# Two stages of a fused attention kernel put into one block, with the key blocks of the first stage in other tiles

## The reference, cut to what matters

```python
x = x + cross_attention(layernorm(x), ctx)       # 16 heads of 128, 4 key heads, RMS norm on queries and keys, softmax
x = x + mixture_of_experts_0(layernorm(x))
x = x + linear_attention(layernorm(x), ctx, mask)  # 16 heads of 16: features relu(f(q)), relu(f(k)) of 64
x = x + mixture_of_experts_1(layernorm(x))
```

## Time and profile before

| | |
|---|---|
| time, median of 3 runs | 1274.75 us (1274.42 to 1274.98) |
| the profiled execution | 1277.79 us |
| its span | 1276.0 us |
| TensorE busy | 1190.6 us, 93% |
| VectorE busy | 879.2 us, 69% |
| ScalarE busy | 738.2 us, 58% |
| GpSimd busy | 536.0 us, 42% |

### The profile page before, as it was taken

The page is one execution under the profiler, slowest core; times in us unless marked ns, Lnnn a source line. Parts: engine busy times, 40 slices in busy tenths (PEclk is TensorE's granted clock), DMA queues, the critical chain, the costliest instruction groups (busy, mean ns, idle before and its releaser), DMA issues.

```text
span 1276.0 us, 28260 instructions
## 1 busy us (share of the span) xinstructions
PE 1190.6 (93%) x10014; PEld 1056.9 (83%) x10014; DVE 879.2 (69%) x1950; ACT 738.2 (58%) x1330; POOL 536.0 (42%) x561
## 2 busy tenths in 40 slices
PE   5999999999877999999999999999999996998888
PEld 4888888888757878888788888887888896887888
DVE  5666666666647888787878878788777644666664
ACT  4656556566555666666576665766666643544432
POOL 2423232233235354463653635535445764633400
PEclk9999999999988999999999999999999998998999
DMA  4211111110031111011001110111001024023000
GB/s 142 75 43 44 53 32 42 54 40 1 2 80 67 49 47 52 1 48 48 19 30 48 48 48 0 48 48 37 11 0 50 18 105 133 2 67 108 1 9 8
DMA packets 42689, 56.12 MB, mean 44 GB/s; under 512 B 3410, under 2 KB 41602, under 8 KB 42626
## 3 DMA queue, kind: packets, MB, share of 16 engines
q1 hardware_dynamic: 41810, 54.23, 13.5%
q10 hardware_dynamic: 816, 1.05, 0.3%
HBM read 54.81 MB, written 0.46 MB: 43 GB/s over the span
## 4 chain that ended last, share of the span: by engine, by line
PE 57%; DVE 7%; DMA 2%; issue 2%; ACT 2%; SPq 1%; POOL 1%; DVEq 0%; ACTq 0%
PE att_bank L104 16%; PE att_bank L106 14%; PE att_bank L105 14%; PE att_bank L1857 6%; PE att_bank L1815 3%; DMA att_raw_n<-in_ctx 1%; DVE att_cn L2112 1%; DVE att_pr L2166 1%; DMA tail_x<-in_x 1%; SPq L1293 1%; DVE tail_full L1431 1%; PE att_bank L1569 1%; DVE tail_hid L1450 0%; PE att_bank L942 0%; PE att_bank L1387 0%
## 5 line engine op out<-in xcount | busy, mean ns | idle before, releaser
L2338 POOL TENSOR_TENSOR att_sq<-att_work,att_sq 128x500 fp32r<-128x500 f32 x90 | 119.8, 1331 | 159.8 <-DVE att_sq L2132 159.8
L2342 POOL TENSOR_TENSOR attention_kk<-att_work,attention_kk 128x500 fp32r<-128x500 f32 x90 | 122.0, 1355 | 153.0 <-DVE attention_kk L2140 153.0
L104 PE MATMUL att_bank<-att_pT,att_cn 125*128 125x448 f32 x384 | 157.1, 409 | 7.2 <-DVE att_pT L2181 6.6
L1995 ACT ACTIVATE att_pr<-att_pr,att_nmx 112x1500 f32<-112x1500 f32 (+1 forms) x96 | 108.5, 1130 | 71.0 <-DVE att_nmx L2169 71.0
L106 PE MATMUL att_bank<-att_pT,att_cn 125*128 125x448 f32 x384 | 140.9, 367 | 0.0
L105 PE MATMUL att_bank<-att_pT,att_cn 125*128 125x448 f32 x384 | 140.4, 366 | 0.0
L2181 DVE TENSOR_TENSOR att_pT<-att_bank,att_pT 125x448 fp32r<-125x448 f32 x192 | 118.1, 616 | 14.5 <-ACT att_pT L2011 14.3
L537 DVE SCALAR_TENSOR_TENSOR attention_kk<-kvs_keys_ps,kvs_bk,attention_kk 64x500 fp32r<-64x500 f32 x96 | 70.9, 738 | 81.5 <-ACT attention_kk L421 79.9
L2166 DVE TENSOR_SCALAR_CACHE_REDUCE att_pr<-att_bank 112x500 f32<-112x500 f32 x192 | 121.7, 675 | 6.3 <-PE att_bank L106 4.9
L1857 PEld LDWEIGHTS att_bank<-all_ident,att_pr 112*125 112x125 f32 x768 | 109.6, 189 | 14.3 <-ACT att_pr L1995 2.3
L292 PE MATMUL kvs_feat<-kvs_f,attention_kk 128*125 128x256 f32 x768 | 112.6, 285 | 6.3 <-DVE attention_kk L537 6.2
(11 more groups left out here) (279 smaller groups left out, 3421.4 us busy)
## 6 DMA issues: line engine op xcount, KB each, us to landing
attention_raw_t<-in_ctxT SPq DMA_DIRECT2D x45, 500.0 KB, 3.9
att_raw_n<-in_ctx SPq DMA_DIRECT2D x16, 750.0 KB
kvs_raw_q<-in_wq SPq DMA_DIRECT2D x8, 256.0 KB, 3.9
tail_wo_raw<-in_wo SPq DMA_DIRECT2D x4, 512.0 KB, 4.4
tail_down_w<-in_down SPq DMA_DIRECT2D x8, 256.0 KB, 4.0
tail_gate_w<-in_gate SPq DMA_DIRECT2D x7, 256.0 KB, 2.9
tail_up_w<-in_up SPq DMA_DIRECT2D x7, 256.0 KB, 3.2
tail_gate_w<-in_gate SPq DMA_DIRECT2D x1, 1760.0 KB, 7.1
```

The source lines that it names most:

```text
L104: nc.tensor.matmul(out, w_lo, x_hi, start=start, stop=False, skip_group_check=True)
L1995: nc.scalar.activation(pr[:, j, keys], pr[:, j, keys], ACT.Exp, scale=-1.0, bias=nmx[:, j:j + 1], accum_out=z[:, 4 * u + j, c:c + 1]).then ...
L2338: nc.gpsimd.tensor_tensor(sq[1][:, i % 2, :], work[:, i % 2, :], sq[0][:, i % 2, :].bitcast(F32), ALU.subtract).then_inc(sq_lo, 1)
L2342: nc.gpsimd.tensor_tensor(kk[:, c, 2 + gi, :], work[:, i % 2, :], kk[:, c, gi, :].bitcast(F32), ALU.subtract).then_inc(k_lo, 1)
```

## The change

- **One block.** `sums_and_queries` returns the five engines' functions instead of making a block; `attention_and_after` calls them at the start of its own. The barrier goes. The waits at the key sums' end (`a_lo`, `k_lo`, `kv_taken`, ...) go too, and the first scores wait for what they need: each chunk's `k_lo`, the queries' `q0_lo`, the last `v_set`. The semaphores of the key sums are cleared by GpSimd after its first attention batch, behind six waits.
- **The last sums.** The turn of the last batch's sums stands in TensorE's order between the second and the third round of scores, and VectorE's `read_blocks` between the third and the fourth.
- **The first rows.** `raw_n` is kept through both stages, its loads stand at the end of SP's list in the key sums, and VectorE rounds three tiles after each of the four rounds of scores (before: none, three, three, six). The weights and tokens that only the start needs lie in the same place.
- **Constants** (`eps`, `mean_mat`, `z`) are set once, at the start; the table load of ScalarE before the attention goes.
- **The last key blocks** start at tile 5 instead of 6, so that all six end within the step.
- **The running key blocks** stand in tiles with `n` of 1 and 3 instead of 0 and 2, each a tile sooner than before: the first half of chunk `c+2` in `n = 3`, the second half of chunk `c+1` in `n = 1`. VectorE's second remainder still follows a tile later. The splits move from `n = 1` to `n = 0`. The query heads keep their tiles.

```diff
-        def keys_at(i, last, t):
+        def keys_at(i, first, last, t):
             c, n = divmod(t, TPC)
             if last:
-                return {0: [(i, 1, 0)], 2: [(i, 1, 1)], 3: [(i, 2, 0)], 5: [(i, 2, 1)]}.get(t, [])
-            if n not in (0, 2):
-                return []
-            return [(i, c + 1, n // 2)] if c + 1 < KC else [(i + 1, 0, n // 2)]
+                return {0: [(i, 1, 1)], 2: [(i, 2, 0)], 4: [(i, 2, 1)]}.get(t, [])
+            if n % 2 == 0:
+                return [(i, 1, 0)] if first and t == 0 else []
+            m = c + (1 if n == 1 else 2)
+            return [(i, m, (3 - n) // 2)] if m < KC else [(i + 1, m - KC, (3 - n) // 2)]
...
-            if n != 1 or (last and c > 0):
+            if n != (1 if first and c == 0 else 0) or (last and c > 0):
...
-        FIRST_KEYS_AT, NK = 6, 2 * KC
+        FIRST_KEYS_AT, NK = 5, 2 * KC
...
+            sp.wait_ge(w_lo, 2)
+            sp.wait_ge(turned_done, DC)
+            for half in range(2):
+                rows = slice(half * (SK // 2), (half + 1) * (SK // 2))
+                sp.dma_start(raw_n[:, half], a["ctx"][0:1, rows, :].rearrange("a (j p) c -> p (a j) c", p=KP))\
+                    .then_inc(n_loaded[half], 16)
+            sp.wait_ge(t_lo, B * KC)
...
-                if n == 0:
-                    pe.wait_ge(proj_free, NH + 1)
-                    pe.wait_ge(ks_lo, 4 * B * KC)
+                if n == 0:
+                    pe.wait_ge(ks_lo, 4 * B * KC)
+                if n == 1:
+                    pe.wait_ge(proj_free, NH + 1)
...
                 for t in range(KT):
                     values(i, t)
+                    if last and t == KT - 1:
+                        key_mean(NK - 1)
                     features(i, t)
...
             add(B - 1, NG - 1)
-            key_mean(NK - 1)
-            turn(B - 1)
...
-        FIRST_ROWS = ((), range(0, 3), range(3, 6), range(6, KT))
+        FIRST_ROWS = (range(0, 3), range(3, 6), range(6, 9), range(9, KT))
...
+                        if j % 2 == 0 and starts:
+                            pe.wait_ge(sums.k_lo, 2 * c + gi + 1)
...
+                            if starts:
+                                pe.wait_ge(sums.q0_lo, 2)
+                                pe.wait_ge(sums.v_set, B * KT)
...
+                    if starts and j == 1:
+                        sums.turn(pe, B - 1)
+                if starts:
+                    pe.wait_ge(sums.kv_done, 4 * B)
+                    pe.wait_ge(sums.kmean_free, NS)
...
             batch(0, False)
+            pool.wait_ge(pv_done, 1)
+            pool.wait_ge(exp_done, 1)
+            pool.wait_ge(ring_free, NSC + 1)
+            for c in range(KC):
+                pool.wait_ge(t_loaded[c], 16)
+            nc.gpsimd.sem_clear(sums.spent)
```

More of the change, by code:

```diff
@@ L1 @@
+import collections
 import math
@@ L221, in run_peeled, with turn, read_blocks, sync @@
             step(B - 1, False, True)
-        @block.sync
-        def _(sp):
+        def turn(pe, i):
+            wait(pe, kv_taken, 4 * (i + 1))
+            for n in range(2):
+                last = nc.tensor.transpose(sums[:, 1, n * 128:(n + 1) * 128], sums_sb[:, n * 128:(n + 1) * 128],
+                                           ident[:])
+            last.then_inc(kv_turned, 1)
+        def read_blocks(dve, i):
+            wait(dve, kv_turned, i + 1)
+            src = sums[:, 1, :].rearrange("p (h n) -> p h n", n=32)
+            to = kv[:, one(context(i))].rearrange("p a h n -> p (a h) n")
+            for n in range(2):
+                r = slice(64 * n, 64 * (n + 1))
+                nc.vector.tensor_tensor(tmp[r], bv[r, :, n, :], src[r, :, HE:RV].to_broadcast([64, NP, HE]),
+                                        ALU.mult).then_inc(tmp_done, 1)
+                nc.vector.tensor_copy(to[r, :, HE], src[r, :, HE]).then_inc(kv_done, 1)
+            for n in range(2):
+                r = slice(64 * n, 64 * (n + 1))
+                wait(dve, tmp_done, 2 * i + n + 1)
+                nc.vector.tensor_tensor(to[r, :, 0:HE], tmp[r], src[r, :, 0:HE], ALU.add).then_inc(kv_done, 1)
+        def sync(sp):
             def load(i, c):
@@ L477, in step @@
                         take_sums(i - 1)
-                    for which in keys_at(i, last, t):
+                    for which in keys_at(i, first, last, t):
                         keys(*which)
@@ L487, in step @@
                         root(h, k)
-                    for which in split_at(i, last, t):
+                    for which in split_at(i, first, last, t):
                         split(*which)
@@ L735, in _ @@
             run_peeled(pool, step)
-            key_low(NK - 1)
-            pool.wait_ge(a_lo, 2)
-            pool.wait_ge(k_lo, NK)
+        numbers = [sem.num for sem in p.sems]
+        spent = range(numbers[0], numbers[-1] + 1)
+        assert numbers == list(spent)
+        for sem in p.sems:
+            nc.release_semaphore(sem)
+        done = Sums(n_loaded, k_lo, q0_lo, kmean_free, v_set, kv_done, turn, read_blocks, spent)
+        return (sync, tensor, scalar, vector, gpsimd), done
 H = 2
@@ L1749, in _ @@
         def _(sp):
+            first[0](sp)
             def load_t(b):
@@ L1831, in output, with scores @@
                 last.then_inc(out_full, 1)
-            def scores(b, u):
+            def scores(b, u, starts=False):
                 for j in range(4):
@@ L1892, in unit, with batch @@
                         wo.spread(pe, B - 1)
-            def batch(b, first, last):
-                scores(b, 0)
-                unit(b, 0, (b, 1), None if first else (b - 1, 1))
+            def batch(b, starts, last):
+                scores(b, 0, starts)
+                unit(b, 0, (b, 1), None if starts else (b - 1, 1))
                 scores(b, 1)
@@ L1971, in _ @@
         def _(act):
+            first[2](act)
             def split_t(b, n):
@@ L2100, in _ @@
         def _(dve):
+            first[3](dve)
             def split_t(b, n):
@@ L2208, in unit, with batch @@
                         split_n(keys[0], t)
-            def batch(b, first, last):
-                before = None if first else (b - 1, 1)
+            def batch(b, starts, last):
+                before = None if starts else (b - 1, 1)
                 scores(b, 0, before)
```

168 lines of the change are left out of this document (72 added, 96 removed).

## The result

The changed kernel takes 1348.3 us (median of four runs, 1348.06 to 1349.21) against 1274.87 us before (four runs on the same chip, 1274.42 to 1275.05): 1.0578 times as long, with a 95% interval of 1.056 to 1.0596. The forecast was 1333 us, range 1300 to 1355. The range held, but two errors partly cancelled: the key sums lost 11 us less than forecast, and the attention loop, to which the prediction gave nothing, lost 25 us.

A forecast was written before the change was run, and what follows sets the result against it. TensorE was taken as the bound, busy 93% of the span. Key waits +51, seam -12 and clock +20 made 58.2 us unrounded; 1277.79 + 58.2 - 3.04 = 1333 us, range 1300 to 1355.

The forecast's parts named there:

- The means: Key sums, tiles 5 and 9: TensorE's mean waits 2.2 us for GpSimd's low squares, twice a step in seven steps.
- E + 3.96: Low squares ready 3.96 us after E, when TensorE issues the instruction after its key matmuls in tiles 5 and 9.
- The other waits: Key sums: waits at tile 1, projections, last passage, first and last steps; with the means, less 6.2 us, +51 us.
- Around tile 1: Six passages into the loop's steps: tile 1's keys wait 2.3 us for VectorE's key low half, 13.8 us together.
- the last passage: Passage into the last step of the key sums, next keys already in tile 0: a wait of 4.0 us.
- the first step: First step of the key sums, tile 1's keys right after tile 0's: an estimated 3.5 us of waiting.
- the loop's projections: Tile 7: the next head's projection waits for the first head's normalisation, 0.6 us once a step.
- The clock: Key sums: half-clock stretches after waits, 11.5 x 1.7 = 20 us, with bounds 0 and 36 us.
- three waits in four: Share of TensorE's waits of about 2 us taken to be followed by 3.4 us at half clock, costing 1.7 us.
- The seam: Last key sum to first product with rows: 12 us gained, bounds 9 and 15; product 16 to 19 us after.
- At no cost: Moved constants, ScalarE's table load, semaphore clearing and first-row loads cost nothing; if the clearing's cover failed, some tenths.
- the clock falls after all: Rival, chance 0.12: every one of the key sums' waits brings a clock fall, 16 us more, 1349 us.

The follow-up runs named there:

- edges_pad16: `queries_first_pad16` with the key blocks of the first and last steps spread over other tiles and both VectorE halves made in the block's own tile there: 1252.4 us.
- queries_first_pad16: The changed kernel with 16 dead VectorE writes at its start and the query heads' work ahead of the key blocks on ScalarE and VectorE: 1255.6 us.
- queries_first_act_pad16: The changed kernel with 16 dead VectorE writes at its start and the query heads' work ahead of the key blocks on ScalarE alone: 1283.6 us.
- fill_pad16: The changed kernel with 16 dead VectorE writes at its start and six extra TensorE matmuls ahead of each of 14 waiting means: 1312.9 us.
- before_pad120: The kernel before the change with 120 dead VectorE writes at its start, its attention loop counted in the trace from instruction 571: 1302.6 us.

## Why the prediction was right, and where it was not

- **The means (2 x 2.2 us in seven steps): right.** 29.5 us measured for 30.8; E + 3.93 for E + 3.96.
- **The other waits: right in place, a little large.** Around tile 1 11.4 us for 13.8, mostly by another way: the sum had tile 1's keys wait for VectorE's key half, and the rows show its features wait for ScalarE's eviction of tile 0's (9.3 us), which stands behind keys, root and weight split. For the rest, the last passage 3.8 for 4.0, the first step 3.2 for 3.5, the loop's projections 3.3 for 4.2. The rows above sum to 54.6 us, those of the same tiles before to 8.8 (6.2 and 1.5 in the earlier trace rows, and 1.1): 46 us for the forecast 51.
- **The clock: right in size, by a rule that was not.** Eleven stretches of about 1.5 us make 16 us; 11.5 of 1.7 were forecast. But they do not follow three waits in four: the first step has one behind both means, the loop's steps behind the second only, and the runs with the same waits differ in this. The wait that ends at 1011.8 us in the earlier trace rows comes back, 1.7 us long, in the other runs; a stretch follows it in `edges_pad16` and not in `queries_first_pad16`. The Trainium skill (TensorE: Matmul & The Clock Gate, "A second HAM failure mode: psum-queue depth-cycling") warned of short idling between groups of matmuls; the trace agrees that short waits can cost the clock and shows that each need not: of the loop's twelve waits of 2.1 us six are followed by a stretch, of the fourteen of 1.5 us in `queries_first_act_pad16` none, and of the six of 1.5 us at tile 1 in `fill_pad16` three.
- **The seam: right.** -13.9 us for -12, within 9 to 15; the product stands 15.2 us after the last sum, a little under the 16 to 19 named. No run separates the barrier from the early rows. Two side remarks were wrong, and the sum uses neither: of the twelve score blocks before, four ran in the half-clock stretch (365.0 to 371.8 us) and not all; and nine casts, each behind a subtraction of 0.75 us, would wait 6.8 us in all and leave a gain of some 7 to 9 us, not 10. The casts cost 0.69 us for three in all four groups.
- **The step that failed is "At no cost".** It priced the writes, table load and clearing that move, by what they do, and not that fewer VectorE instructions ahead of the attention loop move the loop itself. The loop's first instruction stands at 443 in the changed kernel's trace and at 451 before. A loop of 262 traced instructions, a little over two packets of 128, was refetched at each of its five returns where the trace counts its beginning at place 59 of a packet, and not at 51, 65, 67 or 75. The Trainium skill (Runtime: NRT & Kernel Launch, "Instruction fetch mechanics") says that a taken branch whose target is no longer held makes the engine stand until it is fetched, and gives most engines room for 512 instructions, which would be four of these packets. The trace agrees with the first: five packets, and VectorE idle for 3.3 to 3.6 us, at each return. With room for four, a loop lying in three packets would stay with the next one fetched ahead and a loop lying in four would not; that is an argument, which needs the count to be off as said under `before_pad120`, and no run shows how many packets are held.
- **The rivals.** 1349 us, "the clock falls after all", is the measured time but not what happened: the clock fell less often and the rest came from the attention loop. That 1348.3 us lies in the range is luck: without the loop's 28 us the same change takes 1320 us, 13 below the forecast, and what brought it back up was in no term of the sum.

## What to carry to other kernels

Before work is moved to another place in the order, write down for each in-order engine what will stand behind it there, and put what another engine waits for ahead of what only has to be done: here that order on two engines turned a loss of 60 us into a gain of 4. A loop that starts at another place in its engine's program can cost time by that alone; where an unchanged loop grows, look for idle time put down to "issue" at its beginning and for instruction packets in the DMA queues, and try a few dead instructions ahead of it. A sum that comes out right should still be compared stretch by stretch.

## What the hardware showed that was not expected

- Refetching a loop's code on VectorE cost 5.3 to 6.0 us a pass here: VectorE stood idle for 3.3 to 3.6 us, TensorE waited behind it and then ran 6.8 us at half clock. 6 dead instructions cured it in one kernel, 120 brought it on in the other.
- Equal waits of TensorE were followed by a half-clock stretch in one place or run and not in another: of two waits of 2.1 us in each step of the changed kernel's loop only the second was, of two in its first step both were. Where such a stretch of 3.4 us came, it cost about 1.5 us.
